# Attention's query and key projections cut into pieces of three matmuls and dealt out between the scores

## The chip, the cores and the metric

## The reference, cut to what matters

The input is 8 batches of 512 tokens of 512 features. A state-space block and a feed-forward block are computed from the normalised input. The feed-forward block is modulated by an attention of 16 heads of width 32, and only this attention is touched here:

```python
def _attention(x, Wq, Wk, Wv, Wo):
    q = (x @ Wq.T).reshape(b, s, H, HD)          # H = 16, HD = 32, s = 512
    k = (x @ Wk.T).reshape(b, s, H, HD)
    v = (x @ Wv.T).reshape(b, s, H, HD)
    scores = jnp.einsum('bqhd,bkhd->bhqk', q, k) / np.sqrt(HD)
    scores = jnp.where(causal, scores, jnp.finfo(scores.dtype).min)
    probs = jax.nn.softmax(scores, axis=-1)
    out = jnp.einsum('bhqk,bkhd->bqhd', probs, v).reshape(b, s, d)
    return out @ Wo.T
x = _rmsnorm(hidden_states, ln1_w)
attn = _attention(x, Wq, Wk, Wv, Wo)
mod = MOD_SCALE * jnp.tanh(attn @ A)             # A: 512 x 16
gate_pre = h @ W_in_base.T + mod * (h @ A) @ B
```

## The kernel before, in words

The program runs three stages one after the other: the state-space block (to about 900 us of the span), attention (about 900 to 1,720 us) and the feed-forward block. Numbers are kept as a high and a low half, so a product of two full matrices takes three matmuls for each quarter of the inner dimension (high x high, high x low, low x high), and whatever PE leaves in PSUM is first copied by ACT (the high half) and then subtracted by DVE (the low half).

Attention goes over 128 heads, 16 for each of 8 batches. A number g counts the heads; "head i" below is g modulo 16, its place in the batch. A list of steps, written out once by `attn_order(g)` (line 1239), sets the order of work on all engines: each engine walks the same list and does its own part of each step. In turn g:

- "weights" (three parts, p = 0, 1, 2): PE computes the transposed scores of head g (L1433, and a mask with L1435) into PS4 or PS5, ACT takes the exponential into PF (L1516), and after the third part copies PF to the 16-bit tile PH (L1521).
- "largest" (three parts): PE computes the scores of head g + 6 (L1414) into PS2 or PS3, and DVE reduces them to row maxima MX (L1601). PE may fill one of the two banks again only when DVE is through with it.
- "remainder": DVE (three quarters and more) and POOL (the rest) compute PL = PF - PH of head g - 1 (L1608, L1660).
- "mixed", the last step of a turn but one: PE multiplies PH and PL of head g - 1 with the values (20 matmuls of 50 columns, L1450 and L1452) into PS6 and PS7. These two banks collect four heads.
- "summed", after every fourth head, in heads i = 1, 5, 9, 13: ACT copies PS6 and PS7 to AO (L1528), POOL adds (L1667, L1669), DVE divides and sums (L1612 to L1624). It stands in the list behind the three parts of the head and ahead of "mixed", and this "mixed" is the first to write PS6 and PS7 again, so PE waits there for ACT's copy (a_ao, L1441 to L1446).
- "largest_in": for a group of four heads PE turns the maxima round (L1422), ACT negates them into NM (L1508), and SP sends them into row 96 of QS (L1348). The scores of the group's first head wait for its landing (a_nm).
- "modulation", once a batch, for the batch before: PE, ACT, DVE and ACT again in turn (L1459, L1533, L1629, L1535).

The next batch is prepared meanwhile. POOL scales its rows ("scaled"), PE transposes them ("normal", four of them), ACT and DVE split them into RH and RL, and PE projects: "project" makes the queries (n = 0) or keys (n = 1) of a group r of four heads, 12 matmuls of 512 columns in one piece (`project3`, L72 to L74); "values" takes 12 of 256 columns, "low_rank" 12 of 512. ACT and DVE split queries and keys into QT, and SP copies them with 24 DMAs into QS and KS (L1341). SP may do so only when the last score of the same four heads of the current batch has been computed (a_wt, L1337). Behind the fourth group's 24 DMAs SP's list has the load of the next but one batch (STGB, L1327) and the two stores of RH and RL (L1329, L1330), 1 MB each, and then the "largest_in" DMA of group 1.

In a batch the projections stand at the ends of heads 1, 3, 5, ... 15, between the three parts and "mixed": queries and keys by turns. The values stand at the ends of heads 7 to 10, low_rank at head 11, the transposes at the end of head 0 and the start of head 1. All of these use the banks PS0 and PS1 by turns.

## Time and profile before

| | |
|---|---|
| time, median of 3 runs (lowest, highest) | 2844.99 us (2839.48, 2848.57) |
| profiled execution: its own time; its span | 2837.44 us; 2835.6 us |
| busy share of the span: PE, DVE, ACT, POOL | 91%, 50%, 38%, 14% |
| mean granted clock of TensorE | 0.942 |

The page's 40 slices of the span show where PE is busy and at what clock (tenths; the 13th to 25th slice are attention, about 71 us each):

```profile
PE   5899999999994788989889877999999999999997
PEclk8999999999996788999989967999999999999999
```

Shares over the whole span say little about one change, since the three stages have different limits. What counts here is a batch of attention, some 92 us long and nearly the same from one batch to the next.

### The profile page before, as it was taken

The page shows a single profiled execution, that of the slowest core. Times are in us where ns is not written, and L with a number is a line of the kernel's source. Part 1 is how long each engine was busy: PE and PEld are TensorE (multiplying, and loading weights), DVE is VectorE, ACT ScalarE, POOL GpSimd, SP SyncE. Part 2 cuts the span into 40 slices and gives each one's busy share as a digit, 9 for nine tenths or more (in the row PEclk, how much of TensorE's full clock was granted, in tenths as well). Part 3 has the DMA queues.
Part 4 walks back from the last instruction along what each step waited for, and adds up shares of the span by engine and source line. Part 5 has one row for each costly group of instructions (what it writes and reads, how often), then busy time and mean ns, then how long its engine had stood idle before and what let it go on. Part 6 is the DMA issues. An engine that isn't in the chain of part 4 may idle for free.

```text
span 2835.6 us, 38735 instructions
## 1 busy us (share of the span) xinstructions
PE 2584.5 (91%) x14359; PEld 2078.3 (73%) x14359; DVE 1422.6 (50%) x2943; ACT 1091.3 (38%) x1770; POOL 383.8 (14%) x353
## 2 busy tenths in 40 slices
PE   5899999999994788989889877999999999999997
PEld 4677778777774566666667656888888878888886
DVE  6666656656654267676776765221221423333333
ACT  4444444444442166666666663111111211111111
POOL 0000000000001222343334220000000001111111
PEclk8999999999996788999989967999999999999999
DMA  3000000000002444434443313111111322222212
GB/s 128 15 16 16 30 30 1 30 31 15 1 15 93 112 118 113 114 73 114 116 113 74 98 59 113 45 45 45 45 45 45 123 100 90 107 101 89 90 60 75
DMA packets 97728, 194.60 MB, mean 69 GB/s; under 512 B 22128, under 2 KB 22640, under 8 KB 91376
## 3 DMA queue, kind: packets, MB, share of 16 engines
q1 hardware_dynamic: 97536, 192.04, 21.5%
q8 instruction: 120, 1.97, 0.3%
q14 instruction: 72, 0.59, 0.1%
HBM read 99.43 MB, written 41.94 MB: 50 GB/s over the span
## 4 chain that ended last, share of the span: by engine, by line
PE 76%; DVE 10%; ACT 6%; issue 5%; POOL 2%; DMA 1%; SPq 1%; DVEq 0%; ACTq 0%; POOLq 0%
PE PS L72 14%; PE PS L74 14%; PE PS L73 14%; PE PS L1813 4%; PE PS L1815 4%; PE PS L1814 4%; PE PS L1433 2%; PE PS L1414 2%; PE PS L695 2%; PE PS L693 2%; PE PS L694 2%; DVE PL L1608 2%; ACT PF L1516 1%; PE PS L679 1%; PE PS L680 1%
## 5 line engine op out<-in xcount | busy, mean ns | idle before, releaser
L1862 DVE TENSOR_TENSOR GF<-SG,PS 128x512 f32<-128x512 f32 x128 | 88.0, 688 | 619.4 <-PE PS L74 619.4
L1601 DVE CUSTOM_DVE_ANT_0 PS<-PS,MK 128x512 f32<-128x512 f32 (+3 forms) x512 | 240.7, 512 | 41.2 <-PE PS L1414 41.2
L1836 ACT ACTIVATE SG<-PS 128x512 f32<-128x512 f32 x128 | 76.3, 596 | 430.2 <-PE PS L1795 430.2
L1516 ACT ACTIVATE PF<-PS 128x512 f32<-128x512 f32 (+1 forms) x384 | 194.5, 526 | 103.6 <-PE PS L1435 92.0
L1414 PE MATMUL PS<-KS,QS 96*128 96x512 f32 (+3 forms) x512 | 188.1, 412 | 37.9 <-DVE MX L1601 35.6
L1840 ACT CAST GH<-GF 128x512 fp32r<-128x512 f32 x128 | 79.3, 620 | 363.1 <-DVE GF L1862 363.1
L72 PE MATMUL PS<-XH,WH 128*128 128x512 f32 x512 | 211.4, 413 | 6.4 <-DVE XC L967 6.4
L1433 PE MATMUL PS<-QS,KS 97*128 97x512 f32 (+3 forms) x512 | 193.5, 409 | 18.6 <-ACT PF L1516 9.8
L1893 POOL TENSOR_SCALAR XN<-XT,MEAN,RSTD 128x512 f32<-128x512 f32 x32 | 68.1, 2129 | 1041.4 <-DMA M<-m_scratch 726.0
L72 PE MATMUL PS<-FH,GW 128*128 128x512 f32 x512 | 200.4, 391 | 7.7 <-DVE DW L1857 7.7
L1813 PE MATMUL PS<-DW,GH 128*128 128x512 f32 x512 | 200.3, 391 | 5.2 <-DVE GL L1864 5.2
L74 PE MATMUL PS<-XH,WL 128*128 128x512 f32 x512 | 202.6, 396 | 0.0
L73 PE MATMUL PS<-XL,WH 128*128 128x512 f32 x512 | 201.8, 394 | 0.0
L74 PE MATMUL PS<-FH,GW 128*128 128x512 f32 x512 | 201.0, 393 | 0.0
L73 PE MATMUL PS<-FL,UW 128*128 128x512 f32 x512 | 200.8, 392 | 0.0
L74 PE MATMUL PS<-FH,UW 128*128 128x512 f32 x512 | 200.7, 392 | 0.0
L72 PE MATMUL PS<-FH,UW 128*128 128x512 f32 x512 | 200.6, 392 | 0.0
L1814 PE MATMUL PS<-DW,GH 128*128 128x512 f32 x512 | 200.1, 391 | 0.0
L1815 PE MATMUL PS<-DW,GL 128*128 128x512 f32 x512 | 200.1, 391 | 0.0
L73 PE MATMUL PS<-FL,GW 128*128 128x512 f32 x512 | 200.1, 391 | 0.0
L967 DVE SCALAR_TENSOR_TENSOR XC<-PS,CW,XC 128x511 f32<-128x511 f32 (+2 forms) x192 | 143.7, 748 | 49.8 <-ACT XC L821 45.3
L1608 DVE TENSOR_TENSOR PL<-PF,PH 128x1024 f16<-128x1024 f32 x128 | 161.1, 1258 | 9.2 <-ACT PH L1521 9.2
(277 smaller groups left out, 5946.4 us busy)
## 6 DMA issues: line engine op xcount, KB each, us to landing
QS<-QT SPq DMA_DIRECT2D x384, 64.0 KB, 2.0
KS<-QT SPq DMA_DIRECT2D x384, 64.0 KB, 2.0
FH<-rh_scratch SPq DMA_DIRECT2D x16, 1024.0 KB, 5.9
FL<-rl_scratch SPq DMA_DIRECT2D x16, 1024.0 KB, 8.1
XF<-in_x_dram SPq DMA_DIRECT2D x32, 256.0 KB, 4.0
s_scratch<-ZS SPq DMA_DIRECT2D x8, 1024.0 KB, 4.3
STGB<-in_x_dram SPq DMA_DIRECT2D x8, 1024.0 KB, 6.9
rh_scratch<-RH SPq DMA_DIRECT2D x8, 1024.0 KB, 8.6
```

Source lines behind the costliest of these rows:

```text
L72: pe.matmul(o, lh(k), xh(k), start=open_ and k == 0, stop=False, skip_group_check=True)
L73: pe.matmul(o, lh(k), xl(k), start=False, stop=False, skip_group_check=True)
L74: last = pe.matmul(o, ll(k), xh(k), start=False, stop=close and k == nk - 1, skip_group_check=True)
L967: dve.scalar_tensor_tensor(out=y[:, j:], in0=p[:, 0:S - j], scalar=CW[:, d, 3 - j:4 - j], in1=y[:, j:], op0=ALU.mult, op1=ALU.add).then_in ...
L1414: t = pe.matmul(p[:, at:at + n], QS[0:96, h, 128 * k:n], KS[0:96, h, 0:n], start=True, stop=True, skip_group_check=True)
L1433: pe.matmul(p[:, at:at + n], KS[0:97, h, 128 * J:128 * J + 128], QS[0:97, h, 128 * J:512], start=True, stop=False, skip_group_check=True)
L1516: act.activation(PE_[u][:, o:o + at], PS[4 + a % 2][:, 0:at], ACT.Exp, scale=SC).then_inc(a_ex, 1)
L1601: dve.tensor_tensor_reduce(out=p[:, at:at + n], in0=p[:, at:at + n], in1=MK[:, 512 - n:512], scale=1.0, scalar=NEG, op0=ALU.add, op1=ALU.m ...
L1608: dve.tensor_tensor(PL[u][:, 0:1024], PE_[u][:, 0:1024], PH[u][:, 0:1024], ALU.subtract).then_inc(a_rm, 1)
L1813: pe.matmul(PS[4 + k][:, :], GH[g][:, c], DW[0][:, f, :], start=f == 0, stop=False, skip_group_check=True)
L1814: pe.matmul(PS[4 + k][:, :], GH[g][:, c], DW[1][:, f, :], start=False, stop=False, skip_group_check=True)
L1815: t = pe.matmul(PS[4 + k][:, :], GL[g][:, c], DW[0][:, f, :], start=False, stop=f == 7, skip_group_check=True)
```

## The change

A projection is no longer one piece of 12 matmuls but four pieces of three, one for each quarter of the inner dimension. In heads 1 to 14 each of the three parts of a head may be followed by one such piece. The table `thirds` says which: for group r the queries at the parts 3 + 11r to 6 + 11r of the batch (three parts to a head, head i having the parts 3i to 3i + 2), the keys at 8 + 11r to 11 + 11r. The transposes go to heads 15 and 0, the values to heads 4, 5, 8 and 9, low_rank to head 12, the modulation into head 3, all between the parts of a head; POOL's scaling moves to heads 8 to 11. "summed" and "mixed" stay where they are. PS0 now belongs to the projections and two of the transposes, PS1 to everything else.

```diff
+        thirds = {}
+        for r in range(4):
+            for k in range(4):
+                thirds[3 + 11 * r + k] = (r, 0, k)
+                thirds[8 + 11 * r + k] = (r, 1, k)
+
         def attn_order(g):
-            if (g + 15) % 16 == 0 and g + 15 < HEADS:
-                yield "normal", (g + 15) // 16, (2, 3)
-            for i, (Js, ks) in enumerate((((0,), (3,)), ((1, 3), (2, 0)), ((2,), (1,)))):
+            i, nb = g % 16, g // 16 + 1
+            for p, (Js, ks) in enumerate((((0,), (3,)), ((1, 3), (2, 0)), ((2,), (1,)))):
                 if 0 <= g < HEADS:
-                    yield "weights", 3 * g + i, Js
+                    yield "weights", 3 * g + p, Js
...
+                if 3 * i + p in thirds and nb < NB and nb >= 0:
+                    r, n, k = thirds[3 * i + p]
+                    yield "project", 4 * nb + r, (n, k)
+                if p < 2 and i == 0 and 0 <= nb < NB:
+                    yield "normal", nb, 2 + p
+                if p < 2 and i == 15 and 0 <= nb + 1 < NB:
+                    yield "normal", nb + 1, p
+                if p == 1:
+                    if i % 4 == 2 and 0 <= g + 2 < HEADS:
+                        yield "largest_in", (g + 2) // 4, None
+                    if i in (4, 5, 8, 9) and 0 <= nb < NB:
+                        yield "values", nb, (4, 5, 8, 9).index(i)
+                    if i == 12 and 0 <= nb < NB:
+                        yield "low_rank", nb, None
+                    if i == 3 and g >= 19:
+                        yield "modulation", (g - 19) // 16, None
             if g >= 5 and (g - 1) % 4 == 0:
                 yield "summed", (g - 5) // 4, None
...
-            if (g + 15) % 4 == 0 and 0 <= g + 15 < HEADS:
-                yield "project", (g + 15) // 4, 0
-            if (g + 13) % 4 == 0 and 0 <= g + 13 < HEADS:
-                yield "project", (g + 13) // 4, 1
             if 0 <= g - 1 < HEADS:
                 yield "mixed", g - 1, None
...
                 elif kind == "project":
-                    p = own01(kind, a, how)
+                    n, k = how
                     c = slice(128 * (a % 4), 128 * (a % 4) + 128)
-                    pe.wait_ge(a_rl, 4 * (a // 4) + 4)
-                    pe.wait_ge(a_pd, 35)
-                    project3(pe, p[:, :], lambda k: QW[2 * how][:, k, c], lambda k: QW[2 * how + 1][:, k, c],
-                             rh, rl, 4).then_inc(a_pj, 1)
+                    if k == 0:
+                        own01(kind, a, n)
+                        pe.wait_ge(a_rl, 4 * (a // 4) + 4)
+                        pe.wait_ge(a_pd, 35)
+                    p, wh, wl = bank01(kind, a, n), QW[2 * n], QW[2 * n + 1]
+                    pe.matmul(p[:, :], wh[:, k, c], rh(k), start=k == 0, stop=False, skip_group_check=True)
+                    pe.matmul(p[:, :], wh[:, k, c], rl(k), start=False, stop=False, skip_group_check=True)
+                    t = pe.matmul(p[:, :], wl[:, k, c], rh(k), start=False, stop=k == 3, skip_group_check=True)
+                    if k == 3:
+                        t.then_inc(a_pj, 1)
```

On PE, before, at the end of a head that holds a projection: the last part's scores of head g + 6 (KS, QS), all 12 matmuls of the projection (RH or RL with QW; the last eight stand here), and "mixed" (VB with PH and PL).

```order
L73 MATMUL PS<-RL,QW 128x512
L74 MATMUL PS<-RH,QW 128x512
L72 MATMUL PS<-RH,QW 128x512
L73 MATMUL PS<-RL,QW 128x512
L74 MATMUL PS<-RH,QW 128x512
L72 MATMUL PS<-RH,QW 128x512
L73 MATMUL PS<-RL,QW 128x512
L74 MATMUL PS<-RH,QW 128x512
L1450 MATMUL PS<-VB,PH 128x50
```

On PE, now, the end of head 3 of a batch: the modulation's transposes (AM), the third part's scores and mask, and one piece of a projection ahead of "mixed".

```order
L1473 MATMUL PS<-idn,AM 16x128 x4
L1447 MATMUL PS<-QS,KS 128x256
L1449 MATMUL PS<-MR,idb 128x128
L1428 MATMUL PS<-KS,QS 128x256
L1404 MATMUL PS<-RH,QW 128x512
L1405 MATMUL PS<-RL,QW 128x512
L1406 MATMUL PS<-RH,QW 128x512
L1464 MATMUL PS<-VB,PH 128x50
```

Between the last score and "mixed" there were twelve matmuls, and there are three (in head 9, none).

On ACT, before, the end of head 5: three exponentials (PF), the copy to PH, the two copies to AO, and only then the high half of the queries (QT).

```order
L1516 ACTIVATE PF<-PS 128x512 [waits a_rp,a_rm,a_wt]
L1516 ACTIVATE PF<-PS 128x512 [waits a_wt]
L1516 ACTIVATE PF<-PS 128x256 [waits a_wt]
L1521 CAST PH<-PF 128x1280 [waits a_pv,a_ex]
L1528 COPY AO<-PS 128x400 [waits a_sm,a_nu,a_pv]
L1528 COPY AO<-PS 128x400
L1491 CAST QT<-PS 128x512 [waits a_q3,a_pj]
```

On ACT, now, the same head:

```order
L1531 ACTIVATE PF<-PS 128x512 [waits a_rp,a_rm,a_wt]
L1531 ACTIVATE PF<-PS 128x512 [waits a_wt]
L1513 CAST VB<-PS 128x16x16 [waits a_pv,a_fl,a_vl]
L1531 ACTIVATE PF<-PS 128x256 [waits a_wt]
L1536 CAST PH<-PF 128x1280 [waits a_pv,a_ex]
L1506 CAST QT<-PS 128x512 [waits a_q3,a_pj]
L1543 COPY AO<-PS 128x400 [waits a_sm,a_nu,a_pv]
L1543 COPY AO<-PS 128x400
```

The copies to AO still follow the copy to PH, and here the queries' copy and the values' copy (VB) have moved ahead of them.

## Rows read from the trace of the kernel before

**Rows 1.** Busy time by window; us, PE, PEld, DVE, ACT, POOL (count), PEclk, DMA share, GB/s.
```profile
1360.27:1388.10 27.83, 22.77 (x210) 17.52 (x209) 20.16 (x55) 18.61 (x30) 5.69 (x8) 0.98 0.60 180
1388.10:1452.50 64.40, 58.82 (x496) 45.39 (x497) 45.09 (x123) 41.76 (x68) 28.55 (x29) 0.90 0.31 72
...
1402.80:1409.60 6.80, 6.80 (x28) 6.00 (x27) 3.42 (x10) 3.01 (x5) 0.97 (x2) 0.51 0.22 53
```
**Rows 2.** PE's waits, 1388.1 to 1452.5 us: who waited for whom, total us, times, longest.
```profile
PE PS L1414 <- DVE MX L1601: 3.7, 3, 1.7
PE PS L1450 <- DVE PL L1608: 1.6, 3, 0.7
```
**Rows 3.** SP's own queue in order of time, 1355 to 1389 us, and 1452 us.
```profile
1360.27 7.48 SPq L1341 DMA_DIRECT2D QS<-QT  x12
1367.86 8.53 SPq L1341 DMA_DIRECT2D KS<-QT  x12
1376.44 0.58 SPq L1327 DMA_DIRECT2D STGB<-in_x_dram  x1
1377.07 0.53 SPq L1329 DMA_DIRECT2D rh_scratch<-RH  x1
1377.63 0.43 SPq L1330 DMA_DIRECT2D rl_scratch<-RL  x1
1380.62 0.64 SPq L1348 DMA_DIRECT2D QS<-NM  x1
...
1452.46 7.56 SPq L1341 DMA_DIRECT2D QS<-QT  x12
```
**Rows 4.** PE in order of time, idle time before a row in brackets: first score of head 4.
```profile
1388.07 0.47 PE L1433 MATMUL PS<-QS,KS 97*128 97x512 f32 x1 [1.51 <-issue]
...
1480.37 0.47 PE L1433 MATMUL PS<-QS,KS 97*128 97x512 f32 x1 [1.64 <-issue]
```
**Rows 5.** Line 1330 (store of RL): issue to landing over its 8 DMAs.
```profile
DMA to landing us min/median/max: 6.0/10.6/10.9
```
**Rows 6.** PE in order of time: heads 12 and 13 of a batch.
```profile
1345.62 0.20 PE L1450 MATMUL PS<-VB,PH 128*128 128x50 bf16 x1 [0.70 <-DVE PL L1608]
1346.13 0.47 PE L1433 MATMUL PS<-QS,KS 97*128 97x512 f32 x1
...
1347.82 0.38 PE L1414 MATMUL PS<-KS,QS 96*128 96x256 f32 x1
1348.04 0.39 PE L72 MATMUL PS<-RH,QW 128*128 128x512 f32 x1
...
1350.84 0.20 PE L1450 MATMUL PS<-VB,PH 128*128 128x50 bf16 x1
```
**Rows 7.** ACT in order of time: end of head 13.
```profile
1348.40 1.26 ACT L1521 CAST PH<-PF 128x1280 f16<-128x1280 f32 x1
1349.56 0.88 ACT L1528 COPY AO<-PS 128x400 f32<-128x400 f32 x2
1351.04 0.59 ACT L1491 CAST QT<-PS 128x512 fp32r<-128x512 f32 x1 [0.60 <-PE PS L74]
```
**Rows 8.** PE in order of time, last batch (no projections): first and last of four waits.
```profile
1647.66 0.20 PE L1450 MATMUL PS<-VB,PH 128*128 128x50 bf16 x1 [2.29 <-ACT AO L1528]
...
1703.45 0.22 PE L1450 MATMUL PS<-VB,PH 128*128 128x50 bf16 x1 [2.55 <-ACT AO L1528]
```
**Rows 9.** PE in order of time: where clock falls follow.
```profile
1400.42 0.39 PE L1414 MATMUL PS<-KS,QS 96*128 96x256 f32 x1 [1.70 <-DVE MX L1601]
...
1446.90 0.53 PE L1414 MATMUL PS<-KS,QS 96*128 96x256 f32 x1 [1.53 <-DVE MX L1601]
```
**Rows 10.** DVE in order of time, after "summed" of head 1.
```profile
1377.74 0.69 DVE L1584 TENSOR_TENSOR QT<-PS,QT 128x512 fp32r<-128x512 f32 x1
1378.34 0.69 DVE L1601 CUSTOM_DVE_ANT_0 PS<-PS,MK 128x512 f32<-128x512 f32 x1
...
1378.95 1.22 DVE L1608 TENSOR_TENSOR PL<-PF,PH 128x1024 f16<-128x1024 f32 x1
```

More of the change, by code:

```diff
@@ L1260, in attn_order @@
[L1260 to L1265 removed]
+            if (g + 24) % 16 < 4 and g + 24 < HEADS:
+                yield "scaled", (g + 24) // 16, (g + 24) % 16
             if 0 <= g - 1 < HEADS:
                 yield "mixed", g - 1, None
[L1268 to L1269 removed]
@@ L1271, in build @@
-        steps = [w for g in range(-20, HEADS + 4) for w in attn_order(g)]
-        turn01, frees01 = {}, []
+        steps = [w for g in range(-24, HEADS + 4) for w in attn_order(g)]
+        turn01, frees01 = {}, ([], [])
         for kind, a, how in steps:
             if kind == "normal":
-                for d in how:
-                    turn01["normal", a, d] = len(frees01)
-                    frees01.append((a_rl, 4 * a + d + 1))
-            elif kind == "project":
-                turn01[kind, a, how] = len(frees01)
-                frees01.append((a_ql, 2 * a + how + 1))
+                turn01[kind, a, how] = 1 - how % 2, len(frees01[1 - how % 2])
+                frees01[1 - how % 2].append((a_rl, 4 * a + how + 1))
+            elif kind == "project" and how[1] == 0:
+                turn01[kind, a, how[0]] = 0, len(frees01[0])
+                frees01[0].append((a_ql, 2 * a + how[0] + 1))
@@ L1297, in bank01 @@
         def bank01(*what):
-            return PS[turn01[what] % 2]
+            return PS[turn01[what][0]]
         def sm(w, i):
@@ L1323, in attn_sync @@
             for kind, a, how in steps:
-                if kind == "normal" and how[-1] == 3:
+                if kind == "normal" and how == 3:
                     if a + 1 < NB:
@@ L1330, in attn_sync @@
                     sp.dma_start(f32(rl_d[a]), f32(RL[:, :, :])).then_inc(a_rst, 16)
-                elif kind == "project" and how == 1:
+                elif kind == "project" and how == (1, 3):
                     w, r, u = a, a % 4, a % 2
@@ L1374, in own01 @@
             def own01(*what):
-                n = turn01[what]
-                if n >= 2:
-                    pe.wait_ge(*frees01[n - 2])
-                return PS[n % 2]
+                bank, n = turn01[what]
+                if n:
+                    pe.wait_ge(*frees01[bank][n - 1])
+                return PS[bank]
             for kind, a, how in steps:
@@ L1479, in attn_scalar @@
                 if kind == "normal":
-                    for d in how:
-                        act.wait_ge(a_tr, 4 * a + d + 1)
-                        if d == 0 and a:
-                            act.wait_ge(a_rst, 32 * a)
-                            act.wait_ge(a_lr, a)
-                            act.wait_ge(a_pj, 8 * a)
-                        act.copy(RH[:, d, :], bank01(kind, a, d)[:, :]).then_inc(a_rh, 1)
-                elif kind == "project":
-                    act.wait_ge(a_pj, 2 * a + how + 1)
+                    act.wait_ge(a_tr, 4 * a + how + 1)
+                    if how == 0 and a:
+                        act.wait_ge(a_rst, 32 * a)
+                        act.wait_ge(a_lr, a)
+                        act.wait_ge(a_vl, 4 * a)
+                        act.wait_ge(a_pj, 8 * a)
+                    act.copy(RH[:, how, :], bank01(kind, a, how)[:, :]).then_inc(a_rh, 1)
+                elif kind == "project" and how[1] == 3:
+                    n = how[0]
+                    act.wait_ge(a_pj, 2 * a + n + 1)
                     if a >= 2:
-                        act.wait_ge(a_qk[how][(a - 2) % 4], qk_landed(a - 2))
-                    act.copy(QT[how][a % 2][0][:, :], bank01(kind, a, how)[:, :]).then_inc(a_qh, 1)
+                        act.wait_ge(a_qk[n][(a - 2) % 4], qk_landed(a - 2))
+                    act.copy(QT[n][a % 2][0][:, :], bank01(kind, a, n)[:, :]).then_inc(a_qh, 1)
                 elif kind == "values":
```

53 lines of the change are left out of this document (20 added, 33 removed).

## The prediction, made before the changed kernel was run

> **What bounds the kernel now.** The page's slices show attention as the stage where PE has gaps and a clock below full. I read a batch in it by windows first, cut at two events: the last score of a batch's head 15 and the first score of head 4 of the next batch. SP's queue marks the first, since its DMAs QS<-QT for group 3 start when that score is done (1360.27, and 1452.46 one batch later); the row of L1433 at 1388.07 is the second [rows 3, 4]. So a batch is A = 1388.07 - 1360.27 = 27.8 us and B = 1452.46 - 1388.07 = 64.4 us, 92.2 in all. In B PE is busy for 58.8 of 64.4, so idle for 5.6; its mean clock is 0.90 [rows 1]. The low clock is two stretches of 6.8 us (one at 1402.8, as long a one from 1447.2) at 0.51, which is the 1.2 GHz level of the two; each makes 3.4 us of full-speed work last 6.8, so some 3.3 us are lost, 6.7 in B. What remains at 2.4 GHz is 64.4 - 6.7 = 57.7: 52.1 of work and 5.6 of waits, of which DVE causes 5.3 (3.7 ahead of the scores L1414, 1.6 ahead of "mixed") [rows 2]. B is PE's own pace with DVE's interruptions.
>
> A is something else. PE's first score of head 4 waits 1.51 us, in the next batch 1.64, with no engine named [rows 4]. Its exponential's bank had long been free, which leaves the landing of the NM DMA. SP issued that at 1380.62, behind STGB, rh and rl, 1 MB each; rl was issued at 1377.63 and such a store lands a median 10.6 us later, about 1388.2 [rows 3, 5]. PE went on at 1388.07. So A has a floor of its own: 16.2 us for 24 issues (7.48 + 8.53 and gaps), 1.2 to the issue of rl, 10.4 to PE's start, 27.8 us in sum, whatever PE does.
>
> **The change, part by part.** Unit costs at full clock: a head without extras takes 1348.04 - 1345.62 = 2.42 us on PE, a projection 1350.84 - 1348.04 = 2.80, so a piece of three 0.70; "mixed" 1346.13 - 1345.62 = 0.51 [rows 6]. The number of matmuls stays the same.
>
> Work moved between A and B. Before, the projections after heads 15, 1 and 3 lay in A (8.4 us) and five lay in B (14.0). Now the pieces of heads 1 to 3 lie in A (3 + 2 + 3 = 8, 5.6 us) and those of heads 4 to 14 in B (24, 16.8 us). Two of the four transposes of a batch move to head 15 and so from A to B as well, some 0.9 us with their four small matmuls each. Values and low_rank stay in B. B gains 3.7 us of work and A loses 3.7, which its floor doesn't give back. What is left of A for PE: it was busy for 22.8 us there at a clock of 0.98 [rows 1], so 22.2 at full clock, less 3.7 is 18.5 of work; 1.7 for head 1's AO (below); and about 3.8 of waits for DVE (in heads 15 and 0 it has four subtractions of 0.69 more, and the keys of group 0 can't start in PS0 until the queries' subtraction is through). That makes 24.0, 3.8 below 27.8. Those 3.8 become one wait of PE at the first score of head 4, and up to this size anything else in A is free. A stays at 27.8.
>
> The copies to AO. They start when the copy to PH is nearly through, and PE may do "mixed" when they are done: from the last part's L1414 at 1347.82 (the scores before it end where it begins) to 1349.56 + 0.88 = 1350.44 are 2.62 us [rows 6, 7]. Before, L1414 (0.22) and a projection (2.80) covered this, and PE arrived 0.4 us after ACT. Now 0.22 and at most one piece (0.70) do. In the last batch, where there is nothing to project, PE waits here four times, 2.29 to 2.55 us [rows 8], so the wait is real. B has three such places. Head 5: the queries' copy (0.59, which stood behind AO in ACT's list) now stands ahead of it, and the values' copy shifts the last exponential by some 0.2, so 2.62 + 0.59 + 0.2 - 0.92 = 2.5. Head 9, without a piece behind its last part: 2.62 + 0.2 - 0.22 = 2.6. Head 13: 2.62 + 0.15 - 0.92 = 1.8. Together 6.9 us. This is the term that I weigh most. Bounds from both sides: it can't be below 3 x (2.29 - 0.70) = 4.8 if the waits of the last batch hold with a piece each, and not above 3 x 2.55 + 0.59 = 8.2.
>
> The waits for DVE that are there now. After "summed" DVE reaches the next head's maxima late: 1374.42 (AO done) to 1378.34 with a QT subtraction of 0.6 between [rows 10], PE meanwhile having run out of work, 1.70 and 1.53 us at L1414 [rows 9]. Now PE starts that head when AO is done and not 0.4 to 1.8 us later, the subtraction stands elsewhere, and two pieces lie ahead of the third part: PE comes to L1414 at 3.3 (head 6) or 4.0 (10, 14) after AO and is let on at 4.1. Adding the wait for PL that follows (1378.95 + 1.22 = 5.0 after AO with its end) and two of 0.2 to 0.4 at heads 11 and 12, where the keys' subtraction falls between PL and the maxima, I count 2.0 us of such waits in place of 5.6. Bounds: 0 (all hidden) and 5.6 (all stay).
>
> B at full clock: 57.7 + 3.7 + 6.9 + 2.0 - 5.6 = 64.7 us, or between 60.6 and 69.6 with both bounds.
>
> Clock. Waits of 1.70 and 1.53 us were each followed by 6.8 us at the lower level [rows 9, 1], the wait of 1.51 at 1388.07 by none. The changed batch has four waits at least as long: 3.8, 2.5, 2.6, 1.8. I take two falls that are paid in full, as now (6.7 us); bounds none (0) and four (13.4, less some 1.5 that DVE's waits hide).
>
> The Trainium skill, "TensorE: Matmul & The Clock Gate", section "A second HAM failure mode: psum-queue depth-cycling", says that a PE which pauses briefly and often between groups of matmuls swings between its two clock levels, and pays for each swing. That speaks against this change, which turns two covered places into pauses; by that rule more than two falls would be paid, 3.3 us each. The trace agrees in kind: two waits at 1.5 to 1.7 us with a fall behind each.
>
> Everything else. The start of attention: PS0 alone for projections delays the first keys by one copy and one subtraction (0.59 + 0.69), while SP still issues the queries' DMAs (7.48 us), so nothing; bound 1.3 us once. NM of groups 2, 3 and 0: SP's 24 issues (16.2) start with the last score of a group and the fourth head after it comes 21 us later or more, so 2 us are spare, and nothing is charged; bound 1 us each. QT's bank is freed four heads before it is needed. The modulation delays the last exponential of head 3 by some 2 us, inside A's spare 3.8. The last batch and the other stages have the same lists as before.
>
> **The sum.** A batch takes 27.8 + 64.7 + 6.7 = 99.2 us in place of 92.2, 7.0 more. Seven batches are worked on while the next one is prepared: 7 x 7.0 = 49 us. On the profiled execution's 2837.4 us (span 2835.6 and 1.8 around it) that is 2886; on the median of the runs, 7.6 us higher, 2894. The forecast is for the median.
>
> **The rivals.**
>
> 1. *The clock stays up.* The even mixture keeps PE busier around each wait, and no fall follows. Then 27.8 + 64.7 = 92.5 per batch, 0.3 more than now: 7 x 0.3 = 2 us, 2847, no change. For it: not each wait of 1.5 brought a fall. Against it: the new ones are longer.
>
> 2. *PE's order is what counts, and A's floor isn't one.* If the NM DMA lands soon after its issue (2 to 3 us) and PE's two unnamed waits had another cause, A falls to the 24.0 of PE. If then the falls also drop to one and the AO waits stand at their lower bound, a batch is 24.0 + 64.7 - 2.1 + 3.3 = 89.9: 7 x 2.3 = 16 us faster, 2829; with DVE's waits gone too, another 7 x 2.0 = 14, 2815. It decides from the point where A is below 26. For it: in other batches PE came to head 4 without an unnamed wait. Against it: both unnamed waits end 10.4 to 10.7 us after rl's issue. The Trainium skill, "DMA: Bandwidth & Descriptors", section "Queues, rings and completion order", says that DMAs of one queue need not complete in the order of issue, and that a transfer on few engines can be complete before an earlier one on all; by that rule NM could overtake rl, and this rival would hold. The same section has each engine take its descriptors in ring order, which is what the 1.5 us look like.
>
> 3. *Every wait brings the clock down.* Four falls of which 12 us are paid: 27.8 + 64.7 + 12 = 104.5, 12.3 more per batch, 86 us, 2931.
>
> 4. *DVE follows the even stream without effort*, so the waits for it go to 0, and AO's to 4.8, with two falls: 27.8 + 60.6 + 6.7 = 95.1, 2.9 more per batch: 2865. A milder form of the forecast.
>
> **How the numbers follow.** This kernel's runs tell about 0.3% (8.5 us) from no change. Chances: the forecast with its neighbour 4, 0.58; rival 3, 0.10; rival 1, 0.15; rival 2, 0.17. Rival 1 is within 0.3% for two thirds of its chance, the rest on either side, and rival 2 is faster. That makes faster 0.19, same 0.11, slower 0.70. The likeliest case alone spans 2865 to 2915. The range for 8 in 10 leaves out the ends of rivals 2 and 3: 2822 to 2926.
>
> **What would show it.** In the changed profile: PE idle ahead of "mixed" by ACT AO, 1.8 to 2.6 us in heads 1, 5, 9 and 13 of all batches (28 new waits, some 60 us in all); the first score of head 4 still 27 to 29 us after the start of group 3's DMAs, with an unnamed wait of 3 to 4 us; the waits for the maxima (MX ahead of the scores of head g + 6) in B down from 3.7 us to less than half; attention's clock no better than now. The forecast is wrong if A is below 26 us, if B is at or below 61 at full clock, or if the AO waits are under 1 us.

## The result, and the profile after

| | before | after |
|---|---|---|
| median of the runs | 2842.68 us (4 runs) | 2868.42 us (4 runs; 2865.43 to 2870.91) |
| ratio | | 1.0088, 95% interval 1.0067 to 1.0109 |
| profiled span; TensorE's mean clock | 2835.6 us; 0.942 | 2867.0 us; 0.942 |

The change makes the kernel slower by 0.9%, +25.7 us, where +49 was forecast. The profiled execution of the kernel before lies 5.2 us under its median and that of the changed kernel 0.4 above, so the spans of the two profiles differ by 31.4 us.

The windows of the profile after are cut at the same two events as in the prediction: A from SP's first QS<-QT of group 3 to the first score of head 4, B from there to the next such DMA. Columns as in [rows 1]; each pair of rows is one batch's A and B, and the last pair belongs to the last batch that prepares another.

```profile
1282.78:1310.39 27.61, 20.33 (x190) 14.94 (x189) 19.94 (x54) 16.96 (x28) 4.08 (x6) 0.94 0.57 180
1310.39:1379.48 69.09, 62.49 (x516) 47.60 (x516) 45.63 (x124) 41.60 (x70) 27.69 (x30) 0.90 0.28 67
1379.48:1407.25 27.77, 20.19 (x190) 14.90 (x189) 20.43 (x55) 18.20 (x29) 4.76 (x7) 0.93 0.59 177
1407.25:1477.43 70.18, 63.58 (x516) 48.60 (x516) 45.12 (x124) 40.58 (x68) 27.06 (x29) 0.88 0.29 67
...
1573.06:1598.42 25.36, 20.15 (x189) 14.84 (x189) 18.83 (x51) 14.79 (x25) 4.09 (x6) 0.93 0.47 147
1598.42:1664.78 66.36, 58.13 (x514) 43.52 (x509) 46.18 (x125) 42.84 (x72) 18.52 (x26) 0.97 0.31 73
```

Against [rows 1], A is as long as before (27.6 to 27.8, was 27.8) though PE is busy for 2.4 us less in it, and B has grown from 64.4 to 69.1 and 70.2. Only in the last pair is A shorter, 25.4 us: PE comes to the first score of head 4 at 1598.42 without a wait. The start of group 3's DMAs, read for every batch, gives the periods:

| | end of 1st | 2nd | 3rd | 4th | 5th | 6th | 7th | end of the span |
|---|---|---|---|---|---|---|---|---|
| before | 1082.30 | 1174.42 | 1266.95 | 1360.27 | 1452.46 | 1543.41 | 1635.43 | 2835.6 |
| after | 1088.43 | 1187.20 | 1282.78 | 1379.48 | 1477.43 | 1573.06 | 1664.78 | 2867.0 |
| later by | 6.1 | 12.8 | 15.8 | 19.2 | 25.0 | 29.7 | 29.4 | 31.4 |

Five batches in the middle lose 4.7 us each on average (92.2 to 96.9; 3.0 to 6.7 one by one), the first 6.1, the seventh nothing. Those that lose least are the third and fourth, 3.0 and 3.4. There the kernel before has no wait at the first score of head 4 at all (its A is 29.4 and 28.4 us), so A could give something back. It waits there unnamed in three of its seven batches only, and the batch that the prediction read is one of them.

SP's queue and PE at the end of an A, profile after, answering to [rows 3, 4]:

```profile
1379.48 7.48 SPq L1350 DMA_DIRECT2D QS<-QT  x12
1387.07 8.65 SPq L1350 DMA_DIRECT2D KS<-QT  x12
1395.76 0.58 SPq L1336 DMA_DIRECT2D STGB<-in_x_dram  x1
1396.39 0.53 SPq L1338 DMA_DIRECT2D rh_scratch<-RH  x1
1396.96 0.43 SPq L1339 DMA_DIRECT2D rl_scratch<-RL  x1
1397.49 0.83 SPq L1357 DMA_DIRECT2D QS<-NM  x1
```
```profile
1407.25 0.76 PE L1447 MATMUL PS<-QS,KS 97*128 97x512 f32 x1 [3.75 <-issue]
```

NM is issued right behind rl, and PE starts 10.3 us after rl's issue (1396.96), where it was 10.4 before. The unnamed wait is now 3.75 us, as forecast (3.8). In the batch before it the same row reads 2.07 with ACT's exponential named (1310.39 below); it starts 10.25 us after rl too. The name is misleading. PE fills two banks by turns with the parts of a head, so this score needs the bank that ACT's last exponential but one has read. That is the first of these two rows, done at 1305.91, 2.4 us before PE ran out of work:

```profile
1305.31 0.60 ACT L1531 ACTIVATE PF<-PS 128x512 f32<-128x512 f32 x1 [1.31 <-PE PS L1449]
1309.38 0.38 ACT L1531 ACTIVATE PF<-PS 128x256 f32<-128x256 f32 x1
```

The only other semaphore that `weights` waits for at this place and that changes during attention is NM's (a_nm). The batches with ACT's name therefore count as waits for NM too.

PE's waits in the B of 1310.39 to 1379.48, in total and the longest one by one, answering to [rows 2]:

```profile
PE PS L1464 <- ACT AO L1543: 5.5, 3, 2.5
PE PS L1447 <- ACT PF L1531: 2.1, 1, 2.1
PE PS L1404 <- DVE QT L1599: 0.7, 1, 0.7
PE PS L1428 <- DVE MX L1616: 0.3, 1, 0.3
```
```profile
1310.39 0.47 PE L1447 MATMUL PS<-QS,KS 97*128 97x512 f32 x1 [2.07 <-ACT PF L1531]
1324.10 0.20 PE L1464 MATMUL PS<-VB,PH 128*128 128x50 bf16 x1 [2.25 <-ACT AO L1543]
1348.03 0.20 PE L1464 MATMUL PS<-VB,PH 128*128 128x50 bf16 x1 [2.46 <-ACT AO L1543]
1369.40 0.50 PE L1404 MATMUL PS<-RH,QW 128*128 128x512 f32 x1 [0.69 <-DVE QT L1599]
1371.10 0.20 PE L1464 MATMUL PS<-VB,PH 128*128 128x50 bf16 x1 [0.74 <-ACT AO L1543]
```

Two things stand out. The waits for DVE before the scores and before "mixed" (5.3 us in [rows 2]) are down to 0.3, with 0.7 for PS0's subtraction; and three waits for AO have come, 2.25, 2.46 and 0.74. Over all of attention (1000 to 1760 us) AO now takes 57.4 us in 31 waits (9.4 in 4 before, all in the last batch), MX 10.4 (29.5 before), PL 9.8 (19.1 before), and the subtraction that frees PS0 for the next projection 12.2 us in 14 waits, which the kernel before doesn't have.

The clock after, in short windows behind the waits of 2.07, 2.25 and 2.46:

```profile
1311.50:1314.50 3.00, 3.00 (x16) 3.00 (x15) 2.92 (x7) 1.14 (x3) 0.30 (x1) 0.50 0.39 90
1325.50:1330.50 5.00, 5.00 (x19) 3.65 (x19) 4.29 (x10) 2.05 (x5) 0.77 (x2) 0.50 0.01 3
1348.50:1351.50 3.00, 3.00 (x17) 1.99 (x13) 1.84 (x6) 0.60 (x1) 2.92 (x3) 0.53 0.40 96
```

0.50 is the 1.2 GHz level. B has three falls (the next batch's too), not two: but two of the three here are only some 3.4 us long, the third 6.8. The loss is 0.10 x 69.1 = 6.9 us. With the one in A that makes four falls a batch, where the kernel before has two or three, most of them 6.8 us long. Over the five batches in the middle the mean clock is 0.91 in both profiles and PE's busy time the same (412.5 us before, 413.2 now). So nearly all of what these batches lose is idle time of PE, 9.7 us a batch before and 14.3 now.

### The profile page after: what moved, and what is told of

It reads as the page before. It is cut to its first block, busy times and chain, and to the rows that moved or that the text cites. A ratio compares the mean times of both kernels' runs of the same rounds, so it can differ in the third digit from the quotient of the medians.

```text
span 2867.0 us, 38750 instructions
## 1 busy us (share of the span) xinstructions
PE 2580.7 (90%) x14359; PEld 2067.9 (72%) x14359; DVE 1425.4 (50%) x2943; ACT 1080.9 (38%) x1770; POOL 371.9 (13%) x353
## 4 chain that ended last, share of the span: by engine, by line
PE 78%; DVE 8%; ACT 5%; issue 5%; SPq 2%; POOL 1%; DMA 1%; ACTq 0%; DVEq 0%; POOLq 0%
PE PS L72 13%; PE PS L74 12%; PE PS L73 12%; PE PS L1828 4%; PE PS L1830 4%; PE PS L1829 4%; PE PS L1447 3%; PE PS L1428 3%; PE PS L695 2%; PE PS L693 2%; PE PS L694 2%; PE PS L1404 2%; PE PS L1405 2%; PE PS L1406 2%; SPq L1350 2%
## 5 line engine op out<-in xcount | busy, mean ns | idle before, releaser
L1447 PE MATMUL PS<-QS,KS 97*128 97x512 f32 (+3 forms) x512 | 194.8, 412 | 30.4 <-issue 14.7
L1536 ACT CAST PH<-PF 128x1280 f16<-128x1280 f32 x128 | 161.1, 1259 | 4.1
```

Of the source, the lines that this page charges most:

```text
L1447: pe.matmul(p[:, at:at + n], KS[0:97, h, 128 * J:128 * J + 128], QS[0:97, h, 128 * J:512], start=True, stop=False, skip_group_check=True)
L1536: act.copy(PH[u][:, :], PE_[u][:, :]).then_inc(a_ph, 1)
```

## Experiments

Each kernel was run beside the kernel before; ratios are to that, with a 95% interval. The expectations are about which of three things costs: the floor of A (work that is taken out of A is not given back), the copies to AO, or the waits for DVE.

**1. Taking out each suspect.** Two moves, each made in the changed kernel and in the kernel before. "AO move": ACT's copies to AO and POOL's sums are done behind the first part of the head (DVE's part stays), so that they are done well before "mixed" at the end of the head needs PS6 and PS7:

```diff
+                if p == 0 and g >= 5 and (g - 1) % 4 == 0:
+                    yield "collected", (g - 5) // 4, None
...
-                elif kind == "summed":
+                elif kind == "collected":
```

(the last two lines in ACT's and in POOL's walk). "SP move": the load of STGB and the stores of RH and RL follow the NM DMA of group 1.

```diff
-                if kind == "normal" and how == 3:
+                if kind == "normal" and how == 3 and a == 0:
...
                     sp.dma_start(f32(QS[96:97, 4 * r:4 * r + 4, :]), f32(NM[w % 2][:, :])).then_inc(a_nm[r], 16)
+                    if w % 4 == 1 and w // 4 + 1 < NB:
+                        a = w // 4 + 1
+                        if a + 1 < NB:
+                            sp.wait_ge(a_tr, 4 * a + 4)
+                            sp.dma_start(XB, xb_[a + 1]).then_inc(a_st[0], 16)
+                        sp.wait_ge(a_rl, 4 * a + 4)
+                        sp.dma_start(f32(rh_d[a]), f32(RH[:, :, :])).then_inc(a_rst, 16)
+                        sp.dma_start(f32(rl_d[a]), f32(RL[:, :, :])).then_inc(a_rst, 16)
```

The changed kernel with the AO move. Expected:

> The changed kernel, with ACT's copies to AO and POOL's two additions moved from the end of heads 1, 5, 9, 13 to behind the first part of the same head (their inputs are ready since the end of the head before). Theory 1 (the wait of PE for AO is a price of the change, 5.5 us in B besides what it costs in clock, and in A hidden under the landing of NM): the 31 waits of PE for AO (57 us) vanish, B falls by 5 to 8 us a batch, A stays near 27.5; 30 to 45 us faster than the changed kernel (2868), about 2828. Rival (DVE is the real bound behind it, the wait only changes its name): PE waits for the maxima or PL instead, less than 8 us faster.

With the SP move. Expected:

> The changed kernel, with SP's load of the next batch's rows and its two stores of RH and RL (1 MB each) behind the NM DMA of group 1 instead of ahead of it. Theory 1 (A's floor is NM's landing behind these transfers): the wait ahead of the first score of head 4 goes (2 to 4 us, in all batches but the last), A falls from 27.6 to 24 or 25; 3 us x 6 and the 8 us wait of the first batch, 20 to 26 us faster than the changed kernel, about 2845. Rival (the wait has another cause, the exponential of head 3 behind the modulation): A stays within 1 us, no change.

With both. Expected:

> Both moves in the changed kernel. Theory 1: the gains add, and A can now use AO's 1.7 us as well: 55 to 75 us faster than the changed kernel, about 2803, 40 us under the kernel before. Rival (DVE's list is the next bound close behind): less than two thirds of the sum of the two alone.

The kernel before with the AO move. Expected:

> The kernel before, with ACT's copies to AO and POOL's additions behind the first part of heads 1, 5, 9, 13. Theory 1 as it stands after the run of both moves in this kernel (76 us faster): the old place made DVE's sums late, and the waits for the maxima and the clock falls behind them were its price; NM's landing then holds A at 28: B falls by 5 us a batch, A by 0: 30 to 40 us faster than before, about 2808. Rival (both moves are needed together): under 15 us.

With the SP move. Expected:

> The kernel before, with SP's three 1 MB transfers behind the NM DMA of group 1. Theory 1: PE reaches head 4 only 0 to 1.6 us ahead of NM's landing, so little can go: the two waits of 1.5 us and the first batch's 5.5: 5 to 12 us faster than before, about 2835, against 32 us in the changed kernel. Rival (the landing costs both kernels the same): 25 us or more.

With both. Expected:

> The same two moves in the kernel before the change. Theory 1 (the projection covers the copies to AO, and PE reaches head 4 at about NM's landing): only the two waits of 1.5 us for NM and the first batch's (5.5 us) can go, and POOL's additions off DVE's way (1.35 us four times a batch) help a little: 5 to 20 us faster than before, about 2830. Rival (the two moves are good for any order, and the pieces add nothing): as fast as the changed kernel with both moves, within 8 us.

Measured, ratio to the kernel before:

| | kernel before | changed kernel | effect of the change |
|---|---|---|---|
| plain | 1 | 1.0088 [1.0067, 1.0109] | +0.88% |
| AO move | 0.9783 [0.9767, 0.9800], 2785.79 us | 0.9844 [0.9827, 0.9860], 2798.62 us | +0.61% |
| SP move | 0.9992 [0.9983, 1.0002], 2845.34 us | 0.9977 [0.9967, 0.9987], 2835.96 us | -0.15% |
| both | 0.9737 [0.9721, 0.9754], 2767.65 us | 0.9673 [0.9657, 0.9690], 2750.17 us | -0.64% |

For the SP move the mechanism that was expected held, the sizes did not quite: 32 us off the changed kernel where 20 to 26 were expected, and nothing clear off the kernel before where 5 to 12 were. The expectations for the AO move, alone and with the other, were far too small, in both kernels. Read down the last column: the SP move takes 1.0 to 1.25% (29 to 36 us) from the effect of the change, the AO move 0.3 to 0.5% (8 to 14 us). With the floor gone the loss is gone (-0.15% is barely told from nothing), and with both moves the change is a gain. With intervals of 0.1 to 0.2% on each ratio the share of the AO move is barely told from nothing too. So the change's loss hangs on A's floor, and AO, the term that the prediction weighed most, is the lesser cause. Some 5 us of the SP move's share lie in the first batch, where PE's wait at head 4 is 8.0 us in the changed kernel and 5.5 in the kernel before.

What the AO move does in the kernel before can be read from PE's waits over attention (1000 to 1740 us). The maxima fall from 29.5 us to 6.2, and the unnamed waits at head 4 rise from 8.7 to 21.9, because the floor takes back a part of it:

```profile
PE PS L1435 <- issue: 21.9, 6, 4.9
PE PS L1416 <- DVE MX L1603: 6.2, 15, 1.4
```

That A's end hangs on rl's store shows most plainly in the changed kernel with the AO move, where PE comes to the first score of head 4 much earlier and gains nothing. Windows A and B of it, PE's wait, and SP's rl:

```profile
1258.33:1286.07 27.74, 18.44 (x190) 13.86 (x189) 20.36 (x55) 18.10 (x29) 5.67 (x7) 0.95 0.59 184
1286.07:1347.15 61.08, 58.33 (x516) 44.70 (x516) 44.91 (x123) 40.32 (x68) 27.84 (x29) 0.97 0.32 74
```
```profile
1286.07 0.77 PE L1449 MATMUL PS<-QS,KS 97*128 97x512 f32 x1 [7.05 <-issue]
```
```profile
1275.49 0.43 SPq L1341 DMA_DIRECT2D rl_scratch<-RL  x1
```

PE waits 7.05 us and goes on 10.6 us after rl's issue; A is 27.7 us as ever. In this kernel's seventh batch, where only two transfers of 1 MB stand ahead of NM, it goes on 6.6 us after rl's issue and A is 23.0. The changed kernel with the SP move:

```profile
1261.61:1287.02 25.41, 20.21 (x190) 14.90 (x189) 18.84 (x51) 14.81 (x25) 4.08 (x6) 0.93 0.55 159
1287.02:1354.94 67.92, 60.08 (x523) 45.30 (x518) 46.58 (x127) 43.53 (x73) 28.68 (x30) 0.95 0.32 82
```

A is 25.4, and B's clock is 0.95 with the same 5.5 us of waits for AO in it: the fall right behind the first score of head 4 is gone with the wait there. So the floor costs twice, the wait itself and the clock after it. The seventh batch of the changed kernel, whose A carries no load of STGB, says the same without an edit: PE doesn't wait at the first score of head 4, A is 25.4 us, B runs at 0.97 and takes 66.4, and that batch is no slower than before.

How the SP move's gain is made up can be read from the same five batches in the middle. Without it the change adds 22.8 us of idle time to them and next to nothing to PE's busy time (0.7). With it in both kernels the change adds 10.7 us of idle time and takes 13.5 off the busy time, since the clock is now 0.96 against 0.92. By this reckoning the floor accounts for about half of the idle time that the change brings, and the clock for the larger part of what the SP move gives back. Why the clock stays up is not shown beyond the one fall that goes with the wait.

Both moves in the changed kernel, one whole batch, and PE's largest waits in it:

```profile
1211.93:1293.60 81.67, 75.41 (x705) 57.13 (x704) 65.09 (x178) 58.12 (x98) 33.88 (x37) 1.00 0.45 118
```
```profile
PE PS L1438 <- DVE MX L1626: 1.8, 5, 0.4
PE PS L1414 <- DVE QT L1609: 1.6, 3, 0.7
PE PS L1474 <- DVE PL L1633: 1.4, 3, 0.7
PE PS L1457 <- ACT PF L1541: 0.8, 1, 0.8
```

No wait above 0.83 us, and the full clock for the whole batch: 81.7 us in place of 96.9. The kernel before with both moves takes 82.9 to 84.5 a batch and still has one fall of the clock in each (3.4 or 6.8 us long, 2.7 us lost a batch); that is as much as the whole difference between the two.

**2. The cover for AO given back.** The changed kernel with its projections again in one piece of 12 at the ends of heads 1, 3, 5, 7, 9, 11, 13 and 14; the rest stays dealt out.

```diff
-                if 3 * i + p in thirds and nb < NB and nb >= 0:
-                    r, n, k = thirds[3 * i + p]
-                    yield "project", 4 * nb + r, (n, k)
...
+            ends = (1, 3, 5, 7, 9, 11, 13, 14)
+            if i in ends and 0 <= nb < NB:
+                for k in range(4):
+                    yield "project", 4 * nb + ends.index(i) // 2, (ends.index(i) % 2, k)
             if 0 <= g - 1 < HEADS:
```

> The changed kernel with only the pieces undone: each projection again in one piece ahead of mixed, in heads 1, 3, 5, 7, 9, 11, 13 and 14; transposes, values, low_rank, modulation, scaling and banks as in the changed kernel. Theory 1 (the pieces took away the cover of the copies to AO): PE's waits for AO go (57 us to 10), those for the maxima come back (10 to 30 us): 15 to 30 us faster than the changed kernel, about 2845, no worse than before. Rival (the places of the rest, or PS0 alone for projections, are what costs): stays within 8 us of 2868.

Measured: 2872.49 us, ratio 1.0087 [1.0070, 1.0104]: the same as the change. So this expectation failed, and its rival's number came true. PE's waits over attention (1000 to 1740 us) of this kernel:

```profile
PE PS L1429 <- DVE MX L1617: 46.0, 40, 1.8
PE PS L1448 <- issue: 29.0, 6, 7.3
PE PS L1465 <- DVE PL L1624: 21.5, 33, 1.1
PE PS L1465 <- ACT AO L1544: 6.8, 3, 2.3
```

The waits for AO are gone (57.4 to 6.8 us in this window) and those for the maxima and PL are back (18.9 to 67.5); the unnamed ones at head 4 have doubled (14.7 to 29.0). Where PE doesn't wait for ACT's copies to AO, it waits a little later for DVE, whose sums stand behind the same copies. The pieces had traded one for the other.

**3. The pieces alone.** Transposes, values, low_rank, modulation and scaling at the places of the kernel before. In the first version "largest_in" went back to the heads' ends as well.

```diff
-                if p < 2 and i == 0 and 0 <= nb < NB:
-                    yield "normal", nb, 2 + p
...
-                    if i == 12 and 0 <= nb < NB:
-                        yield "low_rank", nb, None
...
+            if (g + 2) % 4 == 0 and 0 <= g + 2 < HEADS:
+                yield "largest_in", (g + 2) // 4, None
```

> The pieces alone: projections in pieces between the scores and the two banks as in the changed kernel, but transposes, values, low_rank, modulation, NM and scaling where the kernel before has them. Theory 1: the pieces carry the loss, 15 to 35 us slower than before, about 2868; values and projections at the head's end in heads 9 and 10 cover some of AO's wait. Rival (the rest carries it): within 8 us of before.

Measured: 2988.5 us, ratio 1.0496 [1.0479, 1.0514]. PE at the first score of head 0, and SP ahead of it:

```profile
1336.65 0.77 PE L1448 MATMUL PS<-QS,KS 97*128 97x512 f32 x1 [15.16 <-issue]
```
```profile
1319.49 7.47 SPq L1351 DMA_DIRECT2D QS<-QT  x12
1327.07 7.49 SPq L1351 DMA_DIRECT2D KS<-QT  x12
1334.65 0.63 SPq L1358 DMA_DIRECT2D QS<-NM  x1
```

The keys of group 3 now end in the third part of head 14, ahead of a "largest_in" at that head's end, so SP had its 24 DMAs ahead of head 0's NM: 15 us a batch. This says nothing of the pieces, only that "largest_in" had to move with them. The second version has "largest_in" between the parts of heads 2, 6, 10 and 14:

> The pieces alone, with the transposes, values, low_rank, modulation and scaling at the places of the kernel before, and the maxima's largest_in between the parts of heads 2, 6, 10, 14 as in the changed kernel. Theory (the loss comes from work moved out of A, whose floor doesn't give it back): the projections' share of that shift is 2.8 of 3.7 us per batch, AO waits as in the changed kernel; 10 to 25 us over the kernel before, near 2863. Rival (the loss lies in the pieces' own AO waits, whatever A does): the same or more than the whole change, 25 to 40 over the kernel before.

Measured: 2861.6 us, ratio 1.0073 [1.0056, 1.0089], +18 us: where the expectation had it, but not by its mechanism: in the batches from 1174.55 us on no wait stands at the first score of head 4 (A 29.7, B 66 us), so the floor doesn't hold this kernel. Its A is PE's own, with a mean clock of 0.83, a wait of 1.7 us for AO in head 1 and one of 1.3 for the subtraction in PS0. The kernel before has neither wait. The pieces alone bring most of the loss, and here by another path than the floor. How much of it is the pieces' and how much the single bank PS0 is not settled: no run gives the changed kernel its two banks back.

**4. Work moved across the edge of A, by itself.** In the kernel before, only the keys of group 3 go from the end of head 15 to the end of head 14: 2.8 us out of A. Alone, and with the SP move.

```diff
-            if (g + 13) % 4 == 0 and 0 <= g + 13 < HEADS:
+            if (g + 13) % 4 == 0 and (g + 13) % 16 != 12 and 0 <= g + 13 < HEADS:
                 yield "project", (g + 13) // 4, 1
+            if (g + 14) % 16 == 12 and 0 <= g + 14 < HEADS:
+                yield "project", (g + 14) // 4, 1
```

> The kernel before with one edit: the keys of group 3 are projected at the end of head 14 in place of head 15, so 2.8 us of PE's work leave A for B, seven times. Theory (A is held by SP's and NM's chain and gives nothing back): B gains 2.8 to 3.7 us, A stays at 28, 15 to 25 us slower than the kernel before. Rival (work is work wherever it stands): within 5 us of the kernel before.

> The same edit with SP's load and two stores of 1 MB behind the NM transfer of group 1, so that A has no floor. Theory: the same shift costs nothing now, within 6 us of the kernel before. Rival (the shift costs by itself, for instance by more maxima waits): 15 to 25 us over the kernel before here too.

Measured: 2837.65 us, ratio 0.9985 [0.9972, 0.9997]; with the SP move 2826.01, 0.9951 [0.9932, 0.9970]. Both expectations failed: the first should have been 15 to 25 us slower (its rival, within 5 us of the kernel before, came true), and the second, which should have been as fast as the kernel before, is faster than the SP move alone (0.9992). A and B of the first, beside [rows 1]:

```profile
1388.02:1451.81 63.79, 59.90 (x508) 46.42 (x508) 44.27 (x123) 41.27 (x67) 28.11 (x29) 0.93 0.31 72
1360.45:1388.02 27.57, 20.78 (x197) 15.85 (x198) 20.88 (x55) 19.07 (x31) 5.24 (x7) 0.92 0.59 181
```
```profile
PE PS L1416 <- DVE MX L1603: 2.9, 3, 1.5
PE PS L1435 <- issue: 2.8, 1, 2.8
PE PS L1452 <- DVE PL L1610: 1.0, 2, 0.7
```

The 12 matmuls are in B (508 for 496) and A is unchanged, with a longer unnamed wait at its end (2.8 us for 1.5), as the theory had it. But B is not longer. 1.4 us were taken up by waits for DVE (5.3 to 3.9), and the clock's loss changed sides: B 0.93 for 0.90, A 0.92 for 0.98, and in A, behind the floor, a slow clock costs nothing. So "work moved out of A costs its length" is wrong as a rule: it costs what the waits and the clock of B don't absorb.

**5. Work moved back into A.** The changed kernel with the values at heads 1 to 4: 4.1 us of PE's work leave B for A.

```diff
-                    if i in (4, 5, 8, 9) and 0 <= nb < NB:
-                        yield "values", nb, (4, 5, 8, 9).index(i)
+                    if i in (1, 2, 3, 4) and 0 <= nb < NB:
+                        yield "values", nb, (1, 2, 3, 4).index(i)
```

> The changed kernel with the values' projections at heads 1 to 4 in place of 4, 5, 8 and 9: three of the four, 3 x 1.4 us of PE's work, leave B for the spare time of A. Theory (A's floor hides them): 15 to 28 us faster than the changed kernel, near 2847, A still 27 to 28.5 us. Rival (A has no spare, its time is PE's own): within 5 us of the changed kernel, A 3 to 4 us longer.

Measured: 2846.6 us, ratio 1.0014 [0.9998, 1.0029], 22 us less than the changed kernel, as expected; but A did not stay at 27 to 28.5 us.

```profile
1176.57:1205.89 29.32, 24.39 (x225) 19.23 (x225) 20.03 (x54) 15.94 (x28) 7.27 (x12) 0.94 0.54 162
1205.89:1272.14 66.25, 57.43 (x487) 41.92 (x482) 45.91 (x124) 42.83 (x70) 25.42 (x24) 0.92 0.31 73
```

A is now 29.3 and PE's own pace, without a wait at head 4. One third of the 22 us comes from the first batch (97.4 to 90.0), whose wait there was the longest; the five in the middle gain 2.1 each, about half of the 4.1 that were moved. Whether the place itself or the filled wait earned this was tried with the SP move, then with both. The pieces alone with both moves were to show what the dealt-out rest is worth.

> The changed kernel with the values at heads 1 to 4 and SP's load and two stores of 1 MB behind the NM transfer of group 1. Theory (the early values were worth 22 us only because they filled a wait of PE for that transfer): with the wait gone they are worth nothing, within 6 us of the 2836 of the same kernel with the values at 4, 5, 8, 9. Rival (they help by themselves): 15 to 25 us less, near 2815.

> The same with ACT's copies to AO and POOL's sums behind the first part of the next head. Theory: within 6 us of the 2750 of the version with the values at 4, 5, 8, 9. Rival: 15 to 25 less, near 2730.

> The pieces alone (transposes, values, low_rank, modulation and scaling at the places of the kernel before), with both moves. Both theories: once neither AO nor NM holds PE, the places of the rest matter little, 2745 to 2765. If it is over 2765, the dealt-out rest is what brings the changed kernel's advantage of 17 us over the kernel before with both moves (2768).

Measured: with the SP move 2838.9 us, 0.9979 [0.9963, 0.9995], against 0.9977 [0.9967, 0.9987] without the early values: they are worth nothing once the floor is gone, as was expected. With both moves 2770.03, 0.9733 [0.9713, 0.9753], some 20 us worse than with the values at their places (0.9673), which neither the expectation nor its rival had. Two of its batches take 86.6 us, the others near 83, where the version without the early values takes 81.7 in each. In all of them a wait has come back at the first score of head 12, 0.8 to 1.6 us long, and in the two long ones the clock is at 0.50 right behind it. SP's queue and PE in one of these:

```profile
1389.00 0.64 SPq L1359 DMA_DIRECT2D QS<-NM  x1
```
```profile
1391.01 0.76 PE L1457 MATMUL PS<-QS,KS 97*128 97x512 f32 x1 [1.46 <-issue]
```

PE goes on 2.0 us after NM's issue in each of five batches (2.4 in the other long one), and that DMA stands in SP's list behind 24 issues of queries and keys. Without the values in heads 8 and 9 PE reaches head 12 ahead of it. This spare time of SP is the one that the prediction had at "2 us". These waits (7 us in six batches) and the two falls (3.4 us of work each) are most of the 20 us.

The pieces alone with both moves: 2776.85, 0.9759 [0.9739, 0.9779], over the 2765 that the expectation named as its bound. So the pieces by themselves are no gain even then, and the dealt-out rest belongs to what brings the changed kernel (0.9673) below the kernel before (0.9737). Their granted clocks go the same way: two falls in most batches with the pieces alone, one in the kernel before, none in the changed kernel, each with both moves. The rest without the pieces was not run with both moves.

## Why the prediction was half right

| step of the prediction | forecast | measured |
|---|---|---|
| A stays at its floor | 27.8 us | 27.3 to 28.5 in six batches, mean 27.8; 25.4 in the seventh |
| wait at the first score of head 4 | 3.8, unnamed | 8.0 in the first batch, then 1.8 to 3.75, none in the seventh; ends 10.2 to 10.9 behind rl's issue |
| AO in B: heads 5, 9, 13 | 2.5, 2.6, 1.8 = 6.9 | 2.25, 2.46, 0.74 = 5.5 |
| waits for DVE in B | 2.0 for 5.6 | 1.0 |
| B at full clock | 64.7 us | 69.1 - 6.9 = 62.2 |
| clock, paid in B | 6.7 us | 6.9 (8.4 in the next batch) |
| a batch | 99.2, +7.0 | 96.9, +4.7 |
| batches that pay in full | 7 | 5 |

The table's rows on B are from the batch of 1282.78 to 1379.48 us. The direction stood, and so did each part of the mechanism. The step that failed is the sum, "99.2 us in place of 92.2, 7.0 more" and "7 x 7.0 = 49 us", in two terms. First, B's waits were set 2.4 us too high: 1.4 for AO, nearly all of it at head 13, where PE first waits 0.69 us for the queries' subtraction in PS0 (1369.40) and by then AO has only 0.74 to go; and 1.0 for DVE, which follows the even stream almost without effort. The prediction had charged nothing in B for PS0 alone. That is rival 4 in half. Second, "7 x 7.0": five batches pay (5 x 4.7 = 23.5), the seventh pays nothing (-0.3) since its A carries no load of STGB and PE reaches head 4 without a wait, and the first batch and the end add 8.2. 31.4 us of span in place of 49; the rest, down to the 25.7 of the medians, is the spread between executions. That the five pay 4.7 on average and not alike has to do with the single batch that was read: where the floor didn't hold in the kernel before, A gave back up to 2.1 us.

The rest of the step on the clock was right in size and wrong in kind. "Two falls that are paid in full" are three, of which two have half the length. And they don't all hang on AO: the one behind the first score of head 4 is the floor's. On the rule of the Trainium skill, "TensorE: Matmul & The Clock Gate", section "A second HAM failure mode: psum-queue depth-cycling", that a PE with brief repeated pauses swings between its clock levels: the trace agrees in kind, with a third fall in B, and not in the price that the prediction set by it (3.3 us for each fall beyond two), since the loss was 6.9 us where 6.7 were lost before. So the forecast of the clock's cost came out right by luck: more falls, and shorter ones.

What the prediction got wrong without its sum showing it is the weight of the causes. It put AO first (6.9 of the +7.0) and set the waits for DVE off against it (-3.6) as though they were another matter. Parts 1 and 2 show them as one chain: the AO move takes 2.2% from the kernel before too, which waits for AO only 9.4 us in all. The trade is nearly even (5.5 for 4.6). What is left of a batch's +4.7 is the 3.7 us of work that A's floor doesn't give back, with the clock behind that floor's wait. The prediction had this term, and its size for the work was right (PE's work in B at full clock is 62.5 - 6.9 = 55.6 us, 3.5 more than the 52.1 before), but part 4 shows that such a term is no constant: the same kind of move cost nothing in the kernel before, where B had waits to fill and PE's longer wait in A took over a slow stretch of the clock. In the changed kernel the waits for DVE were already used up; that this makes the difference is argued from the waits, not shown by a run of its own.

Rival 2 (A's floor isn't one) is refuted: in the changed kernel with the AO move PE stood idle for 7 us and went on 10.6 us after rl's issue. When the 1 MB transfers stood behind NM the wait was gone. The Trainium skill, "DMA: Bandwidth & Descriptors", section "Queues, rings and completion order", says that a transfer's semaphore increment lands only after every earlier write of the same DMA engine; the waits that end 10.2 to 10.9 us after rl's issue agree with that. That a transfer may overtake an earlier one, as the same section allows, no run here shows for NM.

What stays open: by which path the pieces alone lose 18 us (the single bank PS0 has no run of its own), what the rest without the pieces would do with both moves, and why waits of much the same length bring falls of 3.4 us in one place and 6.8 in another.

The best kernel of this study is the changed one with both moves, 2750.17 us, 0.9673 [0.9657, 0.9690] of the kernel before.

## What to carry to other kernels

Cut a period at the points where another chain (here SP's queue and a DMA's landing) sets the time, before you price a reordering: the same matmuls are free on one side and paid on the other, and the waits of engines that hang on one step have to be counted as one, since covering one uncovers the next. If a change that evens out the work makes a kernel slower, try it again with the floor removed before you drop it: here +0.88% turned into -0.15%, and with the second wait gone into -0.64%.

## What the runs showed of the hardware

A small transfer (NM) behind three of 1 MB on one queue let PE go on 10.2 to 11.2 us after the last of them was issued, whether PE had then been idle for 0.6 us or for 8 (kernel before, changed kernel, and the changed kernel and the kernel before with the AO move or with the keys of group 3 moved). Behind two of 1 MB it was 6.6 us (changed kernel with the AO move, seventh batch), and with none right ahead of it PE went on 2.0 us after NM's own issue (both moves and early values).

The granted clock fell from the 2.4 GHz level to the 1.2 GHz level behind waits of 1.3 to 8.0 us, not behind each, and in the changed kernel also three times behind a pair of 0.70 and 0.72 to 0.74 us with 1.7 us between their ends (near 1079, 1273 and 1563 us). So the length of a single wait doesn't tell here whether a fall follows. Most slow stretches lasted some 3.4 or 6.8 us, a few some 10 or 14 (10.4 at 1481 us and 14.0 at 1016.6 in the kernel before). With no wait above 0.83 us the clock stayed at full speed from 1000 to 1558 us (changed kernel with both moves), where the kernel before had two or three falls in each batch and the changed one four in each of five.
